# Latent attention with a tiled mask, one product for sums and values, and folded projections

## The reference

```python
h = _rmsnorm(x, g1)
c = h @ w_down                       # 256 -> 128, the latent
q = _rope(split(c @ wq), pos)        # 16 heads of 8
k = _rope(split(c @ wk), pos)
v = split(c @ wv)
scores = einsum('bhqd,bhkd->bhqk', q, k) / sqrt(8)
scores = where(causal, scores, -inf)
attn = softmax(scores)
o = einsum('bhqk,bhkd->bhqd', attn, v)...reshape(b, s, L)
x = x + o @ w_up                     # 128 -> 256
t = _rmsnorm(x, g2).reshape(-1, D)
probs = softmax(t @ router_w)        # 8 experts, the best 2 are taken
```

## Time and profile before

| what | value |
|---|---|
| median of 3 runs | 939.76 us |
| profiled execution, first to last instruction | 950.8 us |
| TensorE busy | 898.3 us (94%) |
| VectorE, ScalarE, GpSimd busy | 715.1, 608.7, 293.8 us |
| latent stage | to about 221 us |
| first expert tile's transpose | 232.12 us |

### The profile page before, as it was taken

The page is one execution under the profiler, slowest core; times in us unless marked ns, Lnnn a source line. Parts: engine busy times, 40 slices in busy tenths (PEclk is TensorE's granted clock), DMA queues, the critical chain, the costliest instruction groups (busy, mean ns, idle before and its releaser), DMA issues.

```text
span 950.8 us, 24923 instructions
## 1 busy us (share of the span) xinstructions
PE 898.3 (94%) x8496; PEld 805.4 (85%) x8496; DVE 715.1 (75%) x1942; ACT 608.7 (64%) x1694; POOL 293.8 (31%) x359
## 2 busy tenths in 40 slices
PE   5899999887999999999799999999999999999997
PEld 4676677554999999999689898888988989999996
DVE  5768898755666666766889887997878737888867
ACT  4477778763666666666587665866877326677740
POOL 4736665634000000001533434342112102445430
PEclk9999999988999999999999999999999999999999
DMA  8239200062111111133010022021005952333335
GB/s 315 101 112 434 100 23 25 24 245 72 46 51 55 48 56 51 51 135 128 23 35 27 25 87 88 24 89 50 14 20 207 402 141 84 93 100 96 96 106 206
DMA packets 43037, 97.23 MB, mean 102 GB/s; under 512 B 6080, under 2 KB 28480, under 8 KB 41504
## 3 DMA queue, kind: packets, MB, share of 16 engines
q1 hardware_dynamic: 36048, 76.83, 23.1%
q0 software_dynamic: 6864, 18.80, 5.8%
HBM read 62.24 MB, written 33.37 MB: 101 GB/s over the span
## 4 chain that ended last, share of the span: by engine, by line
PE 79%; DVE 10%; DMA 4%; issue 3%; ACT 2%; POOL 1%; another core or an unknown queue 1%; SPq 0%; DVEq 0%; ACTq 0%; POOLq 0%
PE ps L893 23%; PE ps L722 10%; PE ps L724 9%; PE ps L723 9%; PE ps L980 3%; PE ps L990 3%; PE ps L1004 3%; PE ps L815 2%; PE ps L1062 2%; PE ps L829 2%; PE ps L788 2%; PE ps L868 1%; DMA CT<-in_ctxT 1%; DMA BIG<-ys_dram,YI 1%; PE ps L878 1%
## 5 line engine op out<-in xcount | busy, mean ns | idle before, releaser
L722 PE MATMUL ps<-BIGR 128*128 128x256 f32 (+1 forms) x826 | 258.6, 313 | 4.0 <-DVE BIGR L1707 1.0
L893 PE MATMUL ps<-BIG 128*128 128x128 f32 x2000 | 250.7, 275 | 1.1 <-issue 1.0
L893 PEld LDWEIGHTS ps<-BIG 128*128 128x128 f32 x2000 | 237.2, 192 | 1.6 <-issue 1.2
L724 PE MATMUL ps<-BIGR 128*128 128x256 f32 x778 | 221.2, 284 | 0.0
L723 PE MATMUL ps<-BIGR 128*128 128x256 f32 (+1 forms) x602 | 177.1, 294 | 0.0
L722 PEld LDWEIGHTS ps<-BIGR 128*128 128x128 f32 x826 | 157.0, 190 | 12.2 <-issue 6.2
L724 PEld LDWEIGHTS ps<-BIGR 128*128 128x128 f32 x778 | 147.4, 189 | 0.7
L1202 ACT COPY BIG<-BIG 128x512 f32 (+1 forms) x86 | 70.1, 815 | 101.4 <-PE ps L893 78.9
L723 PEld LDWEIGHTS ps<-BIGR 128*128 128x128 f32 x602 | 114.8, 191 | 1.7
L1680 DVE TENSOR_TENSOR BIGR<-BIG,BIGR 128x512 fp32r<-128x512 f32 (+1 forms) x86 | 80.9, 940 | 35.6 <-ACT BIGR L1211 34.9
L1952 POOL DMA_INDIRECT BIG<-ys_dram,YI x32 | 34.8, 1087 | 224.3 <-DMA ys_dram<-BIG 216.0
(11 more groups left out here) (234 smaller groups left out, 1878.1 us busy)
## 6 DMA issues: line engine op xcount, KB each, us to landing
BIG<-in_wgu SPq DMA_DIRECT2D x2, 6144.0 KB
BIG<-in_wd SPq DMA_DIRECT2D x2, 4096.0 KB
BIG<-xs_dram SPq DMA_DIRECT2D x47, 129.5 KB
xs_dram<-CT SPq DMA_DIRECT2D x8, 640.0 KB
BIG<-xs_dram SPq DMA_DIRECT2D x39, 128.0 KB
ys_dram<-BIG SPq DMA_DIRECT2D x39, 128.0 KB, 1.7
BIG<-in_wkv SPq DMA_DIRECT2D x2, 2048.0 KB, 8.9
kv_dram<-BIG SPq DMA_DIRECT2D x16, 256.0 KB, 2.0
```

What stands on the lines that cost most here:

```text
L722: pe.matmul(o, l[0], r[0], start=start, stop=False)
L724: return pe.matmul(o, l[1], r[0], start=False, stop=stop)
L893: i = pe.matmul(o[:, c * 128:(c + 1) * 128], wt[:, at:at + 128], x[:, k * 128:(k + 1) * 128], start=k == 0, stop=k == 1)
```

## The change

Five edits in the latent stage, and a new table of leads.

- **Mask.** The scores of query rows 0 to 63 are only taken with keys 0 to 63. The mask is added by 20 bfloat16 matmuls in the same tiles of 32 by 64 as the scores: a block of -1e30 for the upper right quarter, and two triangles of 32 for each half. The 64 by 64 matmuls of `causal` go.
- **Values and sums.** `v_` holds for each pair of heads a window of 32 columns with the values and a one per head, so one product gives both: 16 matmuls and no `ones_`. `onrm` on VectorE becomes: transpose of 128 by 256 in blocks of 32 out of PSUM, reciprocal of 16 columns, two products of 64 columns, transpose of 128 by 128.
- **Folding.** Once, at the start, `foldT` (four transposes) and `fold` (two matmuls of 384 columns, two of 8) form w_down times wq, wk, wv and w_up times the router, and router columns for the tokens. `qkv` becomes two matmuls of 392 columns straight from `hnT_e`; `wup` has 264 columns, `r` carries the 8 logits along in its last columns. `c`, `c_e`, `tT`, `tT_e` and `log` go.
- **Rotary step.** GpSimd multiplies by minus the sine, and `rope` is one addition of 256 columns.
- **Slots.** The cast of slots to whole numbers moves from VectorE's `rb` to a ScalarE phase `pi`, in both routers; `sc` waits for `pi`. The copy `qkv_e` keeps three ops (values, 8 logits, queries and keys).
- The planner knows a cost for a change of TensorE's tiling; its leads and costs change, and with them the order in the latent stage and in the cross attention. The order inside both expert stages stays.

```diff
-    "V": 100, "V_e": -200, "W": 100, "ah": -300, "al": -300, "btg": 1100, "c_e": -3400, "ch": 800, "cnt": -400,
+    -10000, "kwl": 100, "load_kv": 5100, "load_q": 4800, "load_w0a": 5800, "load_w0b": 5200, "loads": 3300, "max0":
...
     put("strict", p[:, None] < p[None, :])
-    put("neg", np.where(p[None, :] > p[:, None], -1e30, 0.0))
+    put("neg", np.where(p[None, :64] > p[:, None] % 32, -1e30, 0.0))
...
-        add("PE", 220, ("tT", b), ("r", b), ("log", b - 2), banks=[(misc, ("tT_e", b))])
-        add("ACT", 300, ("tT_e", b), ("tT", b), ("log", b - 2))
-        add("PE", 450, ("log", b), ("tT_e", b), banks=[(misc, ("ra", 0, b))])
-        add("DVE", 800, ("ra", 0, b), ("log", b), ("cnt", b - 2), ("rb", 0, b - 4))
+        add("DVE", 550, ("tt", b), ("pow3", b), ("sc", 0, b - 3))
+        add("POOL", 725, ("xr", b), ("r", b))
+        add("DVE", 850, ("ra", 0, b), ("r", b), ("cnt", b - 2), ("rb", 0, b - 4))
         add("PE", 130, ("cnt", b), ("ra", 0, b), banks=[(misc, ("rb", 0, b))])
-        add("DVE", 850, ("rb", 0, b), ("cnt", b))
-        add("POOL", 2550, ("sc", 0, b), ("rb", 0, b), ("tt", b), *[("fill",) for _ in range(b == FILLED)], late=2000)
+        add("DVE", 750, ("rb", 0, b), ("cnt", b))
+        add("ACT", 200, ("pi", 0, b), ("rb", 0, b))
+        add("POOL", 2350, ("sc", 0, b), ("pi", 0, b), ("tt", b), *[("fill",) for _ in range(b == FILLED)], late=2000)
...
+            def foldT():
+                vacant(pe, "foldT")
+                pe.wait_ge(sem("consts_loaded"), 16)
+                pe.wait_ge(sem("small0_loaded"), 16)
+                o = ps("foldT")
+                for k in range(2):
+                    pe.transpose(o[:, k * 128:k * 128 + 128], wdn[:, k, :], ident)
+                for k in range(2):
+                    i = pe.transpose(o[:, 256 + k * 128:384 + k * 128], wup[:, k * 128:k * 128 + 128], ident)
+                i.then_inc(*fills("foldT"))
+            def fold():
+                for k in range(2):
+                    vacant(pe, "fold", i=k)
+                pe.wait_ge(*emptied("foldT"))
+                pe.wait_ge(sem("weights_scaled"), 3)
+                wT = p_[0]
+                for k in range(2):
+                    i = pe.matmul(ps("fold", i=k)[:, 0:384], wT[:, k * 128:k * 128 + 128], wqkv, start=True, stop=True)
+                i.then_inc(*fills("fold", i=1))
+                o = ps("fold", i=0)[:, 384:WIDE]
+                pe.matmul(o, wT[:, 256:384], WQ_[:, 0, 384:WIDE], start=True, stop=False)
+                pe.matmul(o, wT[:, 384:512], WQ_[:, 1, 384:WIDE], start=False, stop=True).then_inc(*fills("fold", i=0))
             def qkv(b):
                 vacant(pe, "qkv", b)
-                pe.wait_ge(*emptied("c", b))
-                pe.matmul(ps("qkv", b)[:, 0:384], cT_[b % 2], wqkv, start=True, stop=True).then_inc(*fills("qkv", b))
+                if b == 0:
+                    for k in range(2):
+                        pe.wait_ge(*emptied("fold", i=k))
+                pe.wait_ge(*emptied("hnT", b))
+                o = ps("qkv", b)[:, 0:WIDE]
+                for k in range(2):
+                    i = pe.matmul(o, hnT_[b % 2][:, k * 128:k * 128 + 128], WQ_[:, k, :], start=k == 0, stop=k == 1)
+                i.then_inc(*fills("qkv", b))
...
+                strips = [slice(32 * g, 32 * g + 32) for g in range(4)]
+                o = [[ps("s", b, i=g)[64 * h:64 * h + 64, :].rearrange("p (n t) -> p n t", n=4) for g in range(4)]
+                     for h in range(2)]
+                for h in range(2):
+                    n = 64 + 64 * h
+                    for g, at in enumerate(strips):
+                        pe.matmul(o[h][g][:, :, 0:n], q[at, 64 * h:64 * h + 64], k[at, :, 0:n], start=True, stop=False)
+                for g, at in enumerate(strips):
+                    pe.matmul(o[0][g][:, :, 64:128], onesb[at, 0:64], mask(at, 63, 64).broadcast_to([32, 4, 64]),
+                              start=False, stop=False)
+                for h in range(2):
+                    for x in range(2):
+                        for g, at in enumerate(strips):
+                            n, lo = 64 - 32 * x, 32 + 32 * g - 32 * x
+                            i = pe.matmul(o[h][g][:, :, 64 * h + 32 * x:64 * h + 64], identw[at, lo:lo + 64],
+                                          mask(at, 0, n).broadcast_to([32, 4, n]), start=False, stop=x == 1)
+                            if h and x:
+                                i.then_inc(*fills("s", b, i=g))
+            def mask(at, lo, hi):
+                return negb[at, lo:hi].rearrange("p (o t) -> p o t", o=1)
...
-                for x in range(2):
-                    for n in range(4):
-                        for g in range(4):
-                            w = v_[b % 3][:, VPAD * g:VPAD * g + VPAD] if x == 0 else ones_
-                            i = pe.matmul(ps("pv", b)[32 * g:32 * g + 32, 128 * x:128 * x + 128],
-                                          w[:, VWIN[n]:VWIN[n] + 32], pt_[g][:, n * 128:n * 128 + 128],
-                                          start=n == 0, stop=n == 3)
+                    pe.wait_ge(sem("sum_columns"), 6)
+                for n in range(4):
+                    x = n // 2
+                    for g in range(4):
+                        at = 128 * g + 64 * x + 24 * (n % 2)
+                        w = v_[b % 3][:, at:at + 32]
+                        i = pe.matmul(ps("pv", b)[32 * g:32 * g + 32, 128 * x:128 * x + 128], w,
+                                      pt_[g][:, n * 128:n * 128 + 128], start=n % 2 == 0, stop=n % 2 == 1)
...
-                pe.wait_ge(*emptied("pv", b))
-                pe.matmul(ps("wup", b)[:, 0:D], oT_[b % 2], wup, start=True, stop=True).then_inc(*fills("wup", b))
-            def tT(b):
-                vacant(pe, "tT", b)
-                pe.wait_ge(*emptied("wup", b))
-                t = r_[b % 2]
-                pe.transpose(ps("tT", b)[:, 0:128], t[:, 0:128], ident)
-                pe.transpose(ps("tT", b)[:, 128:256], t[:, 128:256], ident).then_inc(*fills("tT", b))
-            def log(b):
-                vacant(pe, "log", b)
+                pe.wait_ge(*done("onrm", b))
                 if b == 0:
-                    pe.wait_ge(sem("router_scaled"), 2)
-                pe.wait_ge(*emptied("tT", b))
-                o = ps("log", b)[:, 0:E0]
-                pe.matmul(o, tT_[b % 2][:, 0:128], rt0[:, 0, :], start=True, stop=False)
-                pe.matmul(o, tT_[b % 2][:, 128:256], rt0[:, 1, :], start=False, stop=True).then_inc(*fills("log", b))
+                    pe.wait_ge(*emptied("fold", i=0))
+                pe.matmul(ps("wup", b)[:, 0:D + E0], oT_[b % 2], wupx, start=True, stop=True).then_inc(*fills("wup", b))
...
+            def fold_e():
+                act.wait_ge(*full("fold", i=1))
+                act.mul(WQ_[:, 1, 0:384], ps("fold", i=1)[:, 0:384], g1c[:, 1:2]).then_inc(*frees("fold", i=1))
+                act.wait_ge(*full("fold", i=0))
+                act.mul(WQ_[:, 0, 0:384], ps("fold", i=0)[:, 0:384], g1c[:, 0:1])
+                act.copy(wupx[:, D:D + E0], ps("fold", i=0)[:, 384:WIDE]).then_inc(*frees("fold", i=0))
...
+            def pi(r, b):
+                act.wait_ge(*done("rb", r, b))
+                act.copy(PI[:, b, :], PF[:, b, :]).then_inc(S["slots_whole"], 1)
...
-                v.tensor_tensor(q2[:, :, 0], q2[:, :, 0], m2[:, :, 0], ALU.subtract)
-                v.tensor_tensor(q2[:, :, 1], q2[:, :, 1], m2[:, :, 1], ALU.add).then_inc(S["roped"], 1)
+                v.tensor_tensor(qk_[b % 2], qk_[b % 2], m_[b % 2], ALU.add).then_inc(S["roped"], 1)
...
             def nrm0(b):
+                sums = ot_.rearrange("p (c r) -> p c r", r=32)
                 v.wait_ge(*full("pv", b))
+                v.transpose(ot_, ps("pv", b)[:, 0:256]).then_inc(*frees("pv", b))
+                v.wait_ge(*emptied("pv", b))
+                v.reciprocal(sr_.rearrange("p (c j) -> p c j", c=8), sums[:, :, 16:18]).then_inc(dv, next_step("dve"))
+                then()
+                for x in range(2):
+                    at = slice(4 * x, 4 * x + 4)
+                    v.tensor_tensor(on_.rearrange("p (c x j d) -> p c x j d", c=4, x=2, j=2)[:, :, x, :, :],
+                                    sums[:, at, 0:16].rearrange("p c (j d) -> p c j d", j=2),
+                                    sr_.rearrange("p (c j o) -> p c j o", c=8, o=1)[:, at, :, :].broadcast_to([128, 4, 2, 8]),
+                                    ALU.mult).then_inc(dv, next_step("dve"))
+                then()
                 if b >= 2:
                     v.wait_ge(*full("wup", b - 2))
-                o = oT_[b % 2]
-                v.reciprocal(o, ps("pv", b)[:, 128:256]).then_inc(dv, next_step("dve"))
-                then()
-                v.tensor_tensor(o, ps("pv", b)[:, 0:128], o, ALU.mult).then_inc(*frees("pv", b))
+                v.transpose(oT_[b % 2], on_).then_inc(S["heads_normed"], 1)
...
+            def ra(i, b):
```

(11 more changed lines are left out.)

247 lines of the change are left out of this document (110 added, 137 removed), and 12 rows, old and new, of the table LEAD.

## The result

The changed kernel takes 937.17 us (median of 9 runs, 936.35 to 938.93), the kernel before 939.82 in the same set. The ratio is 0.9968 (95% interval 0.9956 to 0.9979): faster by 0.3%, where 1.5% was forecast. Two later sets on other chips gave 0.9970 (0.9959 to 0.9981) and 0.9980 (0.9969 to 0.9990).

The account below looks back on a forecast made before the run. TensorE was taken to bound the latent stage, VectorE 0.9 us a batch behind. Start +2, batches −9, −4.5, −3.4, last batch −1.5, scatters +2.5 gave −13.9: 925.9 us from 939.76, chance 0.46, range 911 to 938.

Parts of the forecast that it names:

- The forecast's mechanism: Batches 6 to 11: TensorE's saving makes VectorE the bound, period 10.64 to 9.75 us, −4.5 us in all.
- The second rival: Latent stage: the chain through one batch sets the pace, mask slow, start +4, scatters +4; −4, about 936 us; chance 0.19.
- +0.3 for `onrm`: VectorE, per batch: the normalisation's five new ops take about 1.5 us where the old took 1.24.
- one such hit per batch on the products: VectorE's normalisation products, both operands in SBUF, blocked by a GpSimd op: 0.5 us a batch, left out of the forecast.
- The third rival: Latent stage slower: normalisation 2.2 us, products and rotary step caught by GpSimd, 0.5 each a batch; +9, 949 us; chance 0.09.
- VectorE's floor: Middle batches: VectorE's own instructions with their gaps, from 9.7 to 9.45 us a batch, bounds 9.1 and 10.2.
- the first rival: Latent stage: TensorE's saving comes through whole, VectorE's gaps shrink, middle period 9.0 us; −26, or 914 us; chance 0.26.
- Batches 11 to 15: Latent stage: waits govern, TensorE busy for 82%; given the middle's gain, 4 × 0.85 = −3.4 us, bounds 0 and −6.
- Batches 0 to 6: Latent stage: TensorE bound at 96%, its saving comes through nearly whole, −9 us, bounds −4 and −11.
- Start: Before the first scores: the fold waits for the block `small` and adds TensorE work, +2 us, bounds 0 and +4.
- End: Last batch's shorter chain −1.5 us, two more scatters behind the last inverse root +2.5; together +1.
- The base: Whole kernel: −13.9 us from the profiled span of 950.8 carried over to the median, 939.76 − 13.9 = 925.9 us.

Follow-up runs that it names:

- before_third: The kernel before, no edit, profiled again on the faster kind of chip, the same as for a second profile of the changed kernel; median 940.3 us.

## Why the prediction was wrong, by its steps

**The forecast's mechanism was right in the middle.** TensorE's saving moved the bound there to VectorE, whose idle time is nearly gone. With the products unblocked the kernel takes 927.0 us; forecast 925.9. That agreement is in part luck: by stretches it is +1.6, −8.4, −9.3, +0.8, +0.4 and +0.3 against `before_third`, where +2, −9, −4.5, −3.4, +1 and 0 were forecast. The middle gives twice its forecast and batches 11 to 15 nothing. Luck as well are the changed kernel's span of 935.4 and its transpose at 219.0, forecast 936.9 and 218: the base for both was a profile from a slower chip. The second rival named 936 us, near the measured time, but by costs that did not come (a slow mask, +4 at the start, +4 for the scatters).

**The step that failed** is the term "+0.3 for `onrm`" and, in it, "one such hit per batch on the products is 0.5 us, which I don't put into the forecast". There was exactly one such hit in each of the five batches, and it cost 1.1 to 1.3 us, not 0.5: by the means 2 × (0.830 − 0.219) = 1.2 us a batch, or 6.1 in the middle, shown by changing the place of one operand. The whole edit was worth 10.2 us by the medians on two chips, 10.8 side by side on one. I had the mechanism from the earlier trace rows, had named the two SBUF operands as new, and then averaged over GpSimd's busy share. Here the order is fixed, and an instruction meets the same neighbour again and again: the products in seven batches running, and in the kernel before, with an order that alternates, the cast in every second one. So the chance is near 0 or 1 for each place in the order, not a share. The third rival had the products caught, if at 0.5 a batch, and its sign, an `onrm` above 2, came (2.6); the slow transposes that it also wanted did not (0.44 and 0.31 us), and its floor for VectorE was itself too high (next point).

The Trainium skill's rule ("SBUF — State Buffer", section on the two separate sides) says that the loser of the shared ports blocks fully for the other's whole instruction. The trace agrees on the end: the first product of each batch ended 0.09 us after the masking of 1.05 us. That the product lost although its recorded start came first, this rule does not explain. The rotary addition, also out of SBUF alone, took 646 ns in place of 417 in the old order.

**VectorE's floor**, 9.45 us a batch, was too high: with free products the period is 43.86 / 5 = 8.8 at 8.3 busy. Part of what I had counted as its own work was slack between its ops, and part was ops that are shorter in the new order: `tt` takes 470 ns on average, against 633 in the kernel before, and the first layer's scaling (L1421, now L1445) 402 against 587. Here the first rival was nearly right (9.0), and the two errors have opposite signs.

**Batches 11 to 15**, −3.4 forecast, +2.0 measured. This is 5.4 of the 9.3 us by which the sum misses, more than any other stretch, so it is the second step that failed. The 45.73 us of the earlier trace rows included the 7.1 us of "remote" waits; on a chip of the faster kind the kernel before needs 38.04, 9.5 a batch, with TensorE busy for 92%. So the reading "waits govern them, 82%" did not hold there. Why the change then costs 2.0 is only partly shown: the free products give back 1.2 to 2.3 (38.87 and 37.77 in two profiles). The rest is a reading that no run tested. Two of the four batches take 10.84 us each, and in them other short ops of VectorE are long on average, the long ones beside GpSimd's masking, residual or rotary products:

```profile
L1467 DVE TENSOR_SCALAR BIG<-X,st 128x256 f32<-128x256 f32 x2 | 1.6, 776 | 0.0
L1559 DVE TENSOR_TENSOR pr<-OH,RT 128x16 f32<-128x16 bf16 x2 | 1.5, 735 | 0.0
L1536 DVE TENSOR_TENSOR OH<-CS,i 128x16 bf16<-128x16 f32 x3 | 1.3, 440 | 0.1
```

In the kernel before the same three ops take 403, 175 and 176 ns at this place. They stay long with the products out of PSUM (778, 570 and 439).

**Batches 0 to 6**, −9 forecast, −6.3 measured. `pv` takes 118.29 − 117.07 = 1.22 from its start to the next phase, not 1.0, and TensorE's busy share fell from 96% to 90%. With free products it is −8.4, inside the bounds.

**Start**, +2 forecast, +1.5 measured (+0.9 with the second profile): `foldT` waits for `small` until 8.68 us and the first `ctx` starts at 9.56.

**End**, +1 forecast, +1.3 measured (+3.4 in the execution with the clock at 0.77). The casts for three batches stand in one row on ScalarE, long after VectorE had two of them ready, and six scatter issues follow the last residual:

```profile
200.84 0.39 ACT L1205 CAST PI<-PF 128x2 int32<-128x2 f32 x3
```
```profile
206.96 1.06 POOL L1966 DMA_INDIRECT xs_dram<-TT,PI  x1 [0.20 <-issue]
...
213.38 0.96 POOL L1966 DMA_INDIRECT xs_dram<-TT,PI  x1 [0.30 <-issue]
```

**The base.** Carrying −13.9 from a profile 11 us above the median over to the median assumed that the excess was spread evenly or outside. An excess of 11 us in a program whose other runs agree within 0.5 should have made me ask where it lies (the waits of that profile answer it), and widened the bounds of the stretch with the largest waits.

## What to carry to other kernels

When an edit gives VectorE a product with both operands in SBUF, look up which GpSimd instruction stands beside it in the repeating order; if one does, price the whole of it for every turn, and see whether one operand can stay in PSUM. A mean duration well above an op's shortest one is a sign of the same thing, and should not be booked as the op's cost. When a work item is moved to another engine, what counts is what stands ahead of it there: moving the cast (0.17 us when free) to ScalarE, with the rotary edit, cost 21 us in one order, and in another the kernel was 3 us faster with the cast there. And before a difference between two profiles is read, profile one of the kernels twice: one chip was 1.5% slower than another with the same kernel, most of it in one stretch.

## What the runs showed of the hardware

A product of 128 by 64 on VectorE takes 0.21 to 0.22 us free, and 1.30 to 1.54 with both operands in SBUF where GpSimd's masking of 1.05 us starts within 0.4 us behind it; with one operand in PSUM it takes 0.22 there too. A transpose of 128 by 256 in blocks of 32 takes VectorE 444 ns from PSUM to SBUF and 459 from PSUM to PSUM; 128 by 128 inside SBUF takes 311, also beside the masking (at 115.77 above). A reciprocal of 128 by 16 takes 253 ns out of SBUF, also beside a scatter's issue (at 118.69), and one of 128 by 128 out of PSUM 952. Sixteen bfloat16 mask matmuls in tiles of 32 by 64 were through in 0.69 us, partly beside the scores. The same kernel took 940 us on four occasions and 954 to 955 on two, by chip. Of the excess 7.1 us were two waits of VectorE with no named releaser. The first ended at 177 us, 14 us before the fill of the experts' regions was issued (191.2), the second at 200.6 within it, and the fill's own rate was the same on both kinds (381 and 376 GB/s in two windows of 4 us), so the fill alone does not explain them.
